# The denominator product placed directly behind the V product, and the row-maximum matmuls placed in the other slots

## The chip, the cores and the metric

The kernel runs on one core of a Trainium2 chip as one launch. The metric is device time in microseconds. The kernel before takes 3174.51 us, the median of three runs (3169.97 to 3180.08).

## The reference, cut to what matters

Four layers follow each other on 2 x 1024 tokens of width 1024, in fp32: attention, a four-stream mixing layer with Sinkhorn iterations, attention again, and an expert layer. Each layer normalises its input and adds its result to it. The change lies in the two attention layers, which compute

```python
scores = einsum('bqhd,bkhd->bhqk', q, k) / sqrt(HEAD_DIM)      # 32 query heads, 8 key heads, HEAD_DIM 32
scores = where(causal, scores, -inf)
attn = softmax(scores, axis=-1)
out = einsum('bhqk,bkhd->bqhd', attn, v)
```

A softmax needs the maximum of each row of scores, the exponentials, and their sum, the denominator.

## The kernel before, in words

Attention runs batch by batch (2), and in a batch over 8 groups. A group is one key head with its 4 query heads. A group's scores are computed twice. The first time ("S" steps, `row_scores`, L743) they lie with queries on the partitions; VectorE (DVE) takes their row maximum (`maximum`, L599 for tiles on the causal diagonal with the mask added, L602 for the others). The second time ("ST" steps, L790) they lie transposed, with the negated maximum as one more row of the product; ScalarE takes the exponential (L499), and TensorE multiplies the result by V into `ppv` ("PV" step with part 0) and by a matrix of ones into `pden` (part 1, the denominators), both on L810. Each of the two parts is 4 matmuls in the program, one for each head, 32 output columns wide and put on its own quarter of the array; the trace shows 8 records for them.

A group has 12 key tiles ("units" 0 to 11: four for the first 512 queries, eight for the second 512). The list that `iteration` writes has per unit e the steps ST e+1 half 0, ST e+1 half 1, PV e part 0, PV e part 1. All other work is hung behind one of these steps by the table `after`: eight pieces each of the projection of the next queries ("P", L722), the splitting of weights and queries ("HI", "LO", "WS"), stores, and the 38 S steps. The S steps are those of the *next* group (the row maxima must be known before its ST steps), and are spread over the units 1 to 9 in proportion to `columns`, an estimate of how much TensorE does in each step. Every engine walks the same list in the same order and takes out its own steps, so the list sets the order on each engine.

The lists are `body` (with projection and S; 6 groups of a batch), `body6` (S without projection; 1 group) and `body7` or `ahead7` (neither; the last group, `ahead7` prepares the next batch). With 2 layers and 2 batches that is 24, 4 and 4 groups. The six groups of `body` are a hardware loop of 3 turns with 2 groups each. Before the loop a prologue per batch computes keys, values and the first group's maxima.

S steps and projections write into the two banks of the tile `psh`. `bank_plan` gives each step the bank used longest ago; TensorE waits (`sh_free`) until DVE has read the step before it in that bank. Each such step is either one matmul of 512 or 384 columns, two of 256 or four of 128.

Of the kernel before, what the change touches and what calls it, by code (L numbers as in the profile page):

```python
# [30 lines left out]
BANK = 512  # L31
# [19 lines left out]
def unit_offset(e):  # L51

    qc, ki = UNITS[e]
    return max(0, ki * P - qc * BANK)
# [22 lines left out]
def columns(step):  # L77

    what, e, _ = step
    n = BANK - unit_offset(e)  # L80
    return 2 * max(n, BANK // 2) if what == "ST" else 4 * n


def iteration(full_s=True, proj=True, ahead=False):

    steps = [[("ST", e + 1, 0), ("ST", e + 1, 1), ("PV", e, 0), ("PV", e, 1)] for e in range(NU)]
    steps[-1] = steps[-1][2:]  # L90
    after = {step: [] for unit in steps for step in unit}
    first = []
    if proj:
        quarter = lambda c, i: [("P", c, k) for k in range(i * PIECES // 4, (i + 1) * PIECES // 4)]
        first = quarter(0, 0)
        for i, step in enumerate(steps[0][:3]):
            after[step] += quarter(0, i + 1)
        after[steps[0][0]] += [("WS", 0)]
        after[steps[1][1]] += [("HI", 0)]
        after[steps[2][0]] += [("LO", 0)]  # L100
        after[steps[2][0]] += [("WL", 0)]
        after[steps[5][0]] += [("RS", 0)]
        after[steps[10][1]] += quarter(1, 0)
        after[steps[10][2]] += quarter(1, 1) + [("RK", 0)]
        after[steps[10][3]] += quarter(1, 2) + quarter(1, 3)
    if full_s:
        window = [step for unit in steps[1:10] for step in unit]
        total, done, k = sum(map(columns, window)), 0, 0
        for step in window:
            done += columns(step)  # L110
            while k < len(USES) and k * total < done * len(USES) - total // 2:
                after[step] += [("S", k)]
                k += 1
        assert k == len(USES)
        after[steps[10][1]] += [("MT", 0)]
    after[steps[10][1]] += [("NORM", 0)]
    if ahead:


        for i in range(ST_):  # L120
            after[steps[i][0]] += [("XS", i)]
            after[steps[i][2]] += [("XN", i)]
            after[steps[i + 2][1]] += [("XT", i)]
            after[steps[i + 2][2]] += [("XC", i)] + [("XL", i + NX_AHEAD)] * (i + NX_AHEAD < ST_)
        first = [("XL", i) for i in range(NX_AHEAD)]
        for i in range(PIECES):
            after[steps[10][i * 3 // PIECES]] += [("P", "next", i)]
    order = [("ST", 0, 0), ("ST", 0, 1)] + ([("HI", 1), ("LO", 1), ("RS", 1)] if full_s else []) + first
    for unit in steps:
        for step in unit:  # L130
            order += [step] + after[step]
    return order + [("NORM", 1)]


# [55 lines left out]
def attention(nc, sem, layer, x_in, wqkv, cos_in, sin_in, swap, oT_d):  # L190
# [21 lines left out]
    ZT0, W0, SH0, R0, E0, PV0, AC0, N0, ST0, DMA0 = 4, 2, 1, 4, 2, 2, 2, 1, 2, 16  # L212

    pro, body, body6, body7 = prologue(), iteration(), iteration(proj=False), iteration(False, False)
    ahead7 = iteration(False, False, True)
    plan_pro, U_PRO = bank_plan(pro, spare=(2, 3, 4, 5))
    plan = {id(order): bank_plan(order)[0] for order in (body, body6, body7, ahead7)}
# [1664 lines left out]
```

How the kernel before makes its waits and increments, by code:

```python
            def load_w(n, chunk, par):  # L296
                sp.wait_ge(s["w_ready"], n + 1)
                sp.dma_start(wraw[par][:, :, :], wqkv[chunk]).then_inc(w_loaded[par], 16)
# [1 line left out]
            def store_k(b, p):  # L301
                sp.wait_ge(s["q_lo"], b * RB + 2 * p + 2)
                for part in range(2):
                    sp.dma_start(kT_d[part, ds(b, 1), p * P:(p + 1) * P, :].rearrange("o p n -> p (o n)"),
                                 stg[part][:, :].bitcast(F32)).then_inc(s["k_out"], 16)
# [1 line left out]
            def stack_queries(u, par, c):  # L308
                cols = slice(c * BANK, (c + 1) * BANK)
                for part in range(2):
                    sp.dma_start(q_d[par, part, :, cols], stg[part][:, cols].bitcast(F32)).then_inc(s["q_out"], 16)
                sp.wait_ge(s["q_out"], (u + 1) * 32)
                for row, part in enumerate((0, 1, 0)):
                    sp.dma_start(qst[par][row * HD:(row + 1) * HD, :, cols].bitcast(F32),
                                 q_d[par, part, :, cols].rearrange("(h p) n -> p h n", p=HD))\
                        .then_inc(stacked[par][c], 16)
# [6 lines left out]
            def row_max(b, g, par):  # L324
                n = b * NG + g
                sp.wait_ge(s["mT_ready"], n + 1)
                sp.dma_start(m_d[par], mT[:, :]).then_inc(s["m_out"], 16)
                sp.wait_ge(s["m_out"], DMA0 + n * 16 + 16)
                sp.dma_start(qst[par][96:97, :, :].rearrange("o h n -> o (h n)").bitcast(F32),
```

## Time and profile before

| | |
|---|---|
| median of three runs | 3174.51 us |
| the profiled execution | 3168.75 us, span 3167.0 us |
| TensorE busy | 2824.7 us (89%) |
| VectorE busy | 2122.0 us (67%) |
| ScalarE busy | 1003.6 us (32%) |
| mean granted TensorE clock | 0.935 |

Busy shares are means over five stages. The slices of the page show TensorE at nine tenths or more almost everywhere in the two attention layers (slices 2 to 13 and 21 to 34), and another picture in the mixing layer between them. So what a step of attention costs has to be read in a stretch of attention.

### The profile page before, as it was taken

The page shows a single profiled execution, that of the slowest core. Times are in us where ns is not written, and L with a number is a line of the kernel's source. Part 1 is how long each engine was busy: PE and PEld are TensorE (multiplying, and loading weights), DVE is VectorE, ACT ScalarE, POOL GpSimd, SP SyncE. Part 2 cuts the span into 40 slices and gives each one's busy share as a digit, 9 for nine tenths or more (in the row PEclk, how much of TensorE's full clock was granted, in tenths as well). Part 3 has the DMA queues.
Part 4 walks back from the last instruction along what each step waited for, and adds up shares of the span by engine and source line. Part 5 has one row for each costly group of instructions (what it writes and reads, how often), then busy time and mean ns, then how long its engine had stood idle before and what let it go on. Part 6 is the DMA issues. An engine that isn't in the chain of part 4 may idle for free. (4 is left out here: it accounts for less than half of the span.)

```text
span 3167.0 us, 48845 instructions
## 1 busy us (share of the span) xinstructions
PE 2824.7 (89%) x15824; PEld 1810.8 (57%) x15824; DVE 2122.0 (67%) x4647; ACT 1003.6 (32%) x1549; POOL 282.8 (9%) x395
## 2 busy tenths in 40 slices
PE   7999998999999799752868999989999997997999
PEld 6554454654454488652646555446554453785887
DVE  7787787777777433588776877777777784324443
ACT  2243335133344411352521434433234344201000
POOL 1011011001110000000010011010010010001111
PEclk9999999999999899765979999999999998998999
DMA  4323122323131421000133313123223120534111
GB/s 154 93 62 95 52 73 69 112 72 96 52 94 39 138 80 66 0 0 0 79 133 104 90 53 103 53 70 111 84 64 93 52 81 30 192 132 153 67 66 41
DMA packets 121071, 252.90 MB, mean 80 GB/s; under 512 B 12720, under 2 KB 39728, under 8 KB 120880
## 3 DMA queue, kind: packets, MB, share of 16 engines
q1 hardware_dynamic: 120912, 251.03, 25.1%
q8 instruction: 69, 1.13, 0.1%
q14 instruction: 90, 0.74, 0.1%
HBM read 166.57 MB, written 84.41 MB: 79 GB/s over the span
## 5 line engine op out<-in xcount | busy, mean ns | idle before, releaser
L499 ACT ACTIVATE a_prob<-a_pst 128x1024 f32<-128x1024 f32 (+3 forms) x768 | 594.5, 815 | 757.5 <-PE a_pst L790 755.2
L599 DVE CUSTOM_DVE_ANT_0 a_psh<-a_psh,a_edge 128x128 f32<-128x128 f32 (+3 forms) x1024 | 486.8, 513 | 189.1 <-PE a_psh L743 181.8
L743 PE MATMUL a_psh<-a_kst,a_qst 96*128 96x512 f32 (+3 forms) x1536 | 527.0, 404 | 40.2 <-DVE a_mx L599 20.7
L743 PEld LDWEIGHTS a_psh<-a_kst,a_qst 96*128 96x128 f32 x1536 | 263.4, 193 | 480.0 <-DVE a_mx L599 224.9
L790 PE MATMUL a_pst<-a_qst,a_kst 97*128 97x512 f32 (+2 forms) x1536 | 414.0, 372 | 28.0 <-DMA a_qst<-rowmax 10.7
L602 DVE TENSOR_REDUCE a_mx<-a_psh 128x1 f32<-128x512 f32 x512 | 343.5, 688 | 74.5 <-PE a_psh L743 67.5
L810 PE MATMUL a_ppv<-a_prob,a_vg 128*32 128x512 f32 (+3 forms) x3072 | 341.4, 518 | 13.2 <-POOL a_prob L435 11.4
L790 PEld LDWEIGHTS a_pst<-a_qst,a_kst 97*128 97x128 f32 x1536 | 278.5, 200 | 128.5 <-issue 55.5
L810 PE MATMUL a_pden<-a_prob,a_ones 128*32 128x512 f32 (+3 forms) x3072 | 335.2, 509 | 0.0
L435 POOL TENSOR_SCALAR_AFFINE_SELECT a_prob<-a_prob 128x512 f32<-128x512 f32 x256 | 178.7, 698 | 1343.0 <-ACT a_prob L499 1343.0
L646 DVE RECIPROCAL a_dens<-a_dens 128x512 f32<-128x512 f32 x64 | 214.6, 3353 | 66.9 <-ACT a_dens L507 54.5
L722 PE MATMUL a_psh<-a_xT_hi,a_w_hi 128*128 128x512 f32 x416 | 175.2, 421 | 0.6 <-DVE a_xT_lo L570 0.6
L1372 PE MATMUL h_pout<-h_w,h_o 128*128 128x512 f32 x720 | 167.7, 392 | 0.5 <-DVE h_x L1249 0.5
L722 PE MATMUL a_psh<-a_xT_hi,a_w_lo 128*128 128x512 f32 x416 | 165.5, 398 | 0.0
L722 PE MATMUL a_psh<-a_xT_lo,a_w_hi 128*128 128x512 f32 x416 | 165.4, 398 | 0.0
L1372 PEld LDWEIGHTS h_pout<-h_w,h_o 128*128 128x128 f32 x720 | 134.1, 188 | 28.5 <-DMA h_wb<-in_w_branch 0.9
L722 PE MATMUL a_pst<-a_xT_hi,a_w_hi 128*128 128x512 f32 x352 | 142.2, 404 | 6.7 <-DVE a_swp L578 4.5
L599 DVE DVE_READ_ACCUMULATOR2_ANT a_mx<- 128x1 f32 x1024 | 144.2, 141 | 0.0
L722 PE MATMUL a_pst<-a_xT_hi,a_w_lo 128*128 128x512 f32 x352 | 140.3, 399 | 0.0
L722 PE MATMUL a_pst<-a_xT_lo,a_w_hi 128*128 128x512 f32 x352 | 140.1, 398 | 0.0
L810 PEld LDWEIGHTS a_pden<-a_prob,a_ones 128*32 128x32 f32 x3072 | 73.4, 112 | 106.0 <-issue 100.3
L1455 PE MATMUL h_pout<-h_w,h_dg 128*128 x256 | 66.9, 408 | 62.7 <-ACT h_dg L1221 44.9
(212 smaller groups left out, 3798.8 us busy)
## 6 DMA issues: line engine op xcount, KB each, us to landing
a_qst<-q SPq DMA_DIRECT2D x192, 256.0 KB, 4.4
a_wraw<-in_wqkv SPq DMA_DIRECT2D x52, 512.0 KB, 5.7
q<-a_stg_hi SPq DMA_DIRECT2D x64, 256.0 KB, 2.8
q<-a_stg_lo SPq DMA_DIRECT2D x64, 256.0 KB, 3.0
oT<-a_oT SPq DMA_DIRECT2D x64, 256.0 KB, 2.5
a_kst<-kT SPq DMA_DIRECT2D x96, 128.0 KB, 3.1
h_oraw<-oT SPq DMA_DIRECT2D x16, 512.0 KB, 4.0
h_x<-in_x SPq DMA_DIRECT2D x16, 512.0 KB, 4.7
```

Source lines behind the costliest of these rows:

```text
L435: pool.affine_select(out=blk, in_=blk, compare_op=ALU.is_ge, fill=0.0, base=0, pattern=[[0, GH], [1, P]], channel_multiplier=-1)\
L499: act.activation(prob[k % 2][:, 2 * half:2 * half + 2, off:], pst[:, half, :, off:], ACT.Exp, scale=scale).then_inc(s["exp_done"], 1)
L599: part = dve.tensor_tensor_reduce(scores, scores, edge[:, BANK - n:], 1.0, 2 * MASKED, ALU.add, ALU.max, mx_hq[kc][:, h, qt:qt + 1])
L602: part = dve.tensor_reduce(mx_hq[kc][:, heads[0]:heads[0] + m, qt], psh[:, at, 0:m * n].rearrange("p (m n) -> p m n", n=n), AX.X, ALU.max)
L646: dve.reciprocal(dens[:, :], dens[:, :])
L722: mm = pe.matmul(bank(at), w[par][a][:, k, :], xT[x][:, k, c * BANK:(c + 1) * BANK], start=(i == 0), stop=(i == len(passes) - 1))
L743: mm = pe.matmul(psh[:, at, i * n:(i + 1) * n], qst[par][0:96, h, qt * P:(qt + 1) * P], kst[par][0:96, kc * BANK:kc * BANK + n], start=Tru ...
L790: mm = pe.matmul(pst[:, half, hh, off:], kst[par][0:97, ki * P:(ki + 1) * P], qst[par][0:97, 2 * half + hh, qc * BANK + off:(qc + 1) * BAN ...
L810: mm = pe.matmul(acc[h * HD:(h + 1) * HD, off:], lhs, prob[k % 2][:, h, off:], start=(ki == 0), stop=(ki == 4 * qc + 3), skip_group_check= ...
L1372: mm = pe.matmul(pout[:, half, :], o[:, par, a, k, :], w[:, b, k, half * BANK:(half + 1) * BANK], start=(i == 0), stop=(i == len(passes) - 1))
L1455: mm = pe.matmul(pout[:, par, i * C:(i + 1) * C], dg[par][:, i * (NS + 1) + n, :], rhs, start=(n == 0), stop=(n == NS), skip_group_check=True)
```

## The change

After the change a PV step with part 0 is followed at once by part 1 of the same unit, and what hung behind part 0 comes behind part 1. `open_slots` takes the slots behind part 0 out of those over which the S steps are spread, and an ST step counts half more in that spreading than before, so more S steps come behind ST steps.

```diff
     n = BANK - unit_offset(e)
-    return 2 * max(n, BANK // 2) if what == "ST" else 4 * n
+    return 3 * max(n, BANK // 2) if what == "ST" else 4 * n
+
+
+def open_slots(units):
+
+    return [step for unit in units for step in unit if step[0] != "PV" or step[2] == 1]
...
-        window = [step for unit in steps[1:10] for step in unit]
+        window = open_slots(steps[1:10])
...
     for unit in steps:
         for step in unit:
-            order += [step] + after[step]
+            if step[0] == "PV" and step[2] == 0:
+                order += [step]
+            elif step[0] == "PV":
+                order += [step] + after["PV", step[1], 0] + after[step]
+            else:
+                order += [step] + after[step]
```

TensorE in a group of `body`, from the first S step behind unit 4 to the products of unit 5, before. `a_psh<-a_kst,a_qst` is an S step, `a_pst<-a_qst,a_kst` half an ST step:

```order
L743 MATMUL a_psh<-a_kst,a_qst 128x512
...
L790 MATMUL a_pst<-a_qst,a_kst 128x512 x2
...
L743 MATMUL a_psh<-a_kst,a_qst 128x512
...
L790 MATMUL a_pst<-a_qst,a_kst 128x512 x2
...
L743 MATMUL a_psh<-a_kst,a_qst 128x128 x4
...
L810 MATMUL a_ppv<-a_prob,a_vg 32x512 x4
...
L743 MATMUL a_psh<-a_kst,a_qst 128x512
L810 MATMUL a_pden<-a_prob,a_ones 32x512 x4
...
L743 MATMUL a_psh<-a_kst,a_qst 128x512
...
L743 MATMUL a_psh<-a_kst,a_qst 128x512
```

The same place in the changed kernel (line numbers there are 10 higher):

```order
L753 MATMUL a_psh<-a_kst,a_qst 128x512
...
L753 MATMUL a_psh<-a_kst,a_qst 128x512
L798 ISA
L800 MATMUL a_pst<-a_qst,a_kst 128x512 x2
...
L753 MATMUL a_psh<-a_kst,a_qst 128x128 x4
...
L800 MATMUL a_pst<-a_qst,a_kst 128x512 x2
...
L753 MATMUL a_psh<-a_kst,a_qst 128x512
...
L753 MATMUL a_psh<-a_kst,a_qst 128x512
...
L820 MATMUL a_ppv<-a_prob,a_vg 32x512 x4
L820 MATMUL a_pden<-a_prob,a_ones 32x512 x4
```

The S step that stood between the two products is gone from there; between the pair of unit 4 and the pair of unit 5 there are now five S steps in a row of slots (2, 1 and 2 of them, with half an ST step between), where before they were spread over four slots.

The second place is unit 0 of `body`, on TensorE. Before, the last two pieces of the projection (`a_psh<-a_xT`) stand between the two products:

```order
L810 MATMUL a_ppv<-a_prob,a_vg 32x512 x4
L722 MATMUL a_psh<-a_xT_hi,a_w_hi 128x512
...
L722 MATMUL a_psh<-a_xT_hi,a_w_lo 128x512
L810 MATMUL a_pden<-a_prob,a_ones 32x512 x4
...
L790 MATMUL a_pst<-a_qst,a_kst 128x256 x2
...
L743 MATMUL a_psh<-a_kst,a_qst 128x128 x4
```

In the changed kernel they stand behind both:

```order
L820 MATMUL a_ppv<-a_prob,a_vg 32x512 x4
L820 MATMUL a_pden<-a_prob,a_ones 32x512 x4
L732 MATMUL a_psh<-a_xT_hi,a_w_hi 128x512
...
L732 MATMUL a_psh<-a_xT_hi,a_w_lo 128x512
...
L800 MATMUL a_pst<-a_qst,a_kst 128x256 x2
...
L753 MATMUL a_psh<-a_kst,a_qst 128x128 x4
```

The projection of a group thus ends one denominator product later, and the first S step comes after one half of the ST step and not after both. The order on DVE within a group stays the same.

## Rows read from the trace of the kernel before

**Rows 1.** Busy us of each engine in a group of each kind, and two other stretches.

```profile
core 0: us, PE busy (x) PEld busy (x) DVE busy (x) ACT busy (x) POOL busy (x), PEclk, DMA share, GB/s
179.19:232.91 53.72, 53.16 (x341) 27.86 (x338) 43.66 (x100) 22.20 (x31) 6.45 (x9) 1.00 0.29 81
232.91:293.09 60.18, 57.73 (x338) 30.49 (x338) 43.38 (x100) 22.61 (x31) 5.92 (x9) 0.91 0.25 66
463.00:466.00 3.00, 1.60 (x8) 0.78 (x12) 2.74 (x3) 3.00 (x5) 0.63 (x1) 1.00 0.30 89
...
250.00:258.00 8.00, 8.00 (x44) 4.46 (x37) 3.75 (x12) 3.38 (x5) 0.63 (x1) 0.50 0.72 210
```

**Rows 2.** Timeline of PE, unit 5: start us, us, engine line op, xcount.

```profile
203.79 0.56 PE L743 MATMUL a_psh<-a_kst,a_qst 96*128 96x128 f32 x4
204.28 1.06 PE L810 MATMUL a_ppv<-a_prob,a_vg 128*32 128x512 f32 x8
205.27 0.50 PE L743 MATMUL a_psh<-a_kst,a_qst 96*128 96x512 f32 x1
205.70 1.06 PE L810 MATMUL a_pden<-a_prob,a_ones 128*32 128x512 f32 x8
206.70 0.72 PE L743 MATMUL a_psh<-a_kst,a_qst 96*128 96x512 f32 x2
207.26 0.62 PE L790 MATMUL a_pst<-a_qst,a_kst 97*128 97x512 f32 x2
207.98 0.50 PE L743 MATMUL a_psh<-a_kst,a_qst 96*128 96x512 f32 x1
208.32 0.63 PE L790 MATMUL a_pst<-a_qst,a_kst 97*128 97x512 f32 x2
```

**Rows 3.** Timeline of PE in the last group of a batch (ahead7), products side by side.

```profile
546.37 1.07 PE L810 MATMUL a_ppv<-a_prob,a_vg 128*32 128x512 f32 x8
547.25 1.04 PE L810 MATMUL a_pden<-a_prob,a_ones 128*32 128x512 f32 x8
548.22 0.97 PE L790 MATMUL a_pst<-a_qst,a_kst 97*128 97x384 f32 x4
```

**Rows 4.** Timeline of DVE, the row maxima in the same group as rows 2.

```profile
204.53 0.30 DVE L599 CUSTOM_DVE_ANT_0 a_psh<-a_psh,a_edge 128x128 f32<-128x128 f32 x1 [0.32 <-PE a_psh L743]
...
205.25 0.33 DVE L599 CUSTOM_DVE_ANT_0 a_psh<-a_psh,a_edge 128x128 f32<-128x128 f32 x1
...
207.23 1.98 DVE L602 TENSOR_REDUCE a_mx<-a_psh 128x1 f32<-128x512 f32 x3 [0.73 <-PE a_psh L743]
...
210.81 0.43 DVE L599 CUSTOM_DVE_ANT_0 a_psh<-a_psh,a_edge 128x256 f32<-128x256 f32 x1 [0.56 <-PE a_psh L743]
...
211.54 2.88 DVE L602 TENSOR_REDUCE a_mx<-a_psh 128x1 f32<-128x512 f32 x4
215.25 0.57 DVE L599 CUSTOM_DVE_ANT_0 a_psh<-a_psh,a_edge 128x384 f32<-128x384 f32 x1 [0.83 <-PE a_psh L743]
```

**Rows 5.** Timeline of PE, where units of that group begin and end.

```profile
192.25 0.51 PE L743 MATMUL a_psh<-a_kst,a_qst 96*128 96x256 f32 x2 [0.38 <-DVE a_mx L599]
...
195.89 0.34 PE L743 MATMUL a_psh<-a_kst,a_qst 96*128 96x384 f32 x1
...
201.70 0.90 PE L743 MATMUL a_psh<-a_kst,a_qst 96*128 96x512 f32 x2
...
223.97 0.50 PE L743 MATMUL a_psh<-a_kst,a_qst 96*128 96x512 f32 x1
...
226.36 0.28 PE L752 MATMUL a_psh<-a_ident,a_mx 128*32 128x128 f32 x1
```

**Rows 6.** Timeline of PE at the start of a group behind the loop's branch.

```profile
245.39 0.50 PE L743 MATMUL a_psh<-a_kst,a_qst 96*128 96x256 f32 x2 [1.02 <-DVE a_swp L578]
...
247.96 0.50 PE L743 MATMUL a_psh<-a_kst,a_qst 96*128 96x256 f32 x2 [1.28 <-DVE a_mx L599]
```

**Rows 7.** Waits of PE, the whole span: who for whom, us in total, times, longest.

```profile
PE a_psh L743 <- DVE a_mx L599: 20.7, 42, 1.3
```

## The prediction

> **What bounds the kernel now.** I read the busy time of one group of each kind first, then the PE timeline inside it, then the DVE timeline beside it, then PE's waits. In a plain `body` group of 53.72 us PE is busy 53.16 us at full clock, and DVE 43.66 us [rows 1]. So TensorE is the bound, with a second engine at 81% behind it. The two are coupled by the two banks of `psh`: S step k can start only when DVE has taken the maximum of S step k-2. In the whole span PE waited for the masked maxima of L599 only 42 times, 20.7 us in all [rows 7], because the S steps are spread evenly enough. The change takes work off TensorE and bunches the S steps, so both sides have to be worked out.
>
> **What the change saves on PE.** An S step between the two products costs 0.43 us from its start to the next product (205.27 to 205.70), and two of them plus nothing else take 0.56 us to the next ST step (206.70 to 207.26) [rows 2]. A product of 512 columns that is followed by full-width work takes 1.00 us (204.28 to 205.27, 205.70 to 206.70). Side by side the first takes 0.88 us (546.37 to 547.25) and the second 0.97 (547.25 to 548.22) [rows 3], 1.85 for the pair. Split, the same work is 1.00 + 0.43 + 1.00 = 2.43 us. Joined it is 1.85, and the S step elsewhere costs 0.24 (an ordinary slot: 208.32 less 207.98 is 0.34 behind a wait, and the second S of a pair takes 0.56 - 0.34 = 0.22). That is 0.34 us less per split removed. A `body` group has ten splits (units 0, 1, 2, 4 to 10), a `body6` group eight; the last group of a batch has none. 24 x 10 + 4 x 8 = 272 splits, so 272 x 0.34 = 92 us if nothing else happened.
>
> The skill has the cause of this as a rule: by the Trainium skill, "TensorEngine Tiling (Array Packing)", section "Key Properties", changing the tiling mode drains TensorE, while the tiles of one mode run beside each other. The trace agrees with it, 1.00 against 0.88 and 0.34 against 0.22 us. By this rule alone the time would be 3169 - 92 = 3077 us; that is the first rival below.
>
> **What it costs: waits for a bank.** DVE's side first. A plain maximum (L602) starts 0.53 us after its S step (206.70 to 207.23), three of them take 1.98 us, so one starts 0.65 after the other; the S step of 207.98 is the one that needs the bank of 206.70, and it starts 1.28 us after it, 0.75 after DVE's start [rows 2, 4]. The four-head maximum starts 0.74 after its S step (203.79 to 204.53) and its last pass ends at 205.58, so it frees its bank 1.05 + 0.06 = 1.11 us after its start. The two-head one holds DVE 0.73 (210.81 to 211.54), and by the same 0.10 on top frees after 0.83. The 384-column one frees after 0.57 + 0.06 = 0.63 [rows 4].
>
> Now unit 5 as the changed list has it, with t = 0 at the first S step behind the products of unit 4. S13 at 0, S14 at 0.34, the ST half at 0.57, S15 could start at 1.04 but waits for S13's bank until 1.28 (wait 0.24). Its four matmuls take 0.49, as behind any break; ST half at 1.77, S16 at 2.24, S17 could start at 2.48. It needs the bank of S15, whose maximum starts at 1.28 + 0.74 = 2.02 and frees at 3.13: wait 0.65. S17 to the product takes 0.43, so 3.56, and the pair 1.85: the next unit begins at 5.42. Of this 0.89 us are waits, against 0.34 us that the join saved.
>
> The other units by the same ledger. Unit 6: S20 waits 0.24, S22 waits for the two-head maximum until 2.80; 5.09 us. Unit 7: waits 0.24 and 0.31; 4.82. Unit 8: S30 waits 0.46, S31 0.16, S32 0.11; 4.83. Unit 9: S35 waits 0.47; to S37 3.73. From S13 to S37 that is 23.89 us; before it was 202.04 (the second of the two at 201.70) to 223.97, 21.93 [rows 5]. So +1.96. From S6 to S13 (units 3 and 4), S8 waits 0.37, S11 0.51 and S12 0.28: 7.18 us against 202.04 - 195.89 = 6.15, +1.03. From S2 to S6 the ledger gives 3.77 against 195.89 - 192.25 = 3.64, +0.13.
>
> The start of a group: the last two projection pieces now stand behind the denominators, which puts their end 0.85 us later (1.85 - 1.00). DVE's rotation of that projection stands in front of the first maxima, and S1 and S2 already wait for DVE (0.38 at 192.25) [rows 5], so this passes on in part. Bounds 0 and 0.85, I take 0.45, for the savings in units 0 and 1 then end in a wait. The end: the last two S steps now come as a pair, so S37's maximum is done one maximum's remainder later. Before, 2.39 us lay between S37 and the transpose of the maxima (223.97 to 226.36) [rows 5]; I get 2.66, +0.27. Unit 10 has no S steps, its join is a clean -0.33. PE's other partners see nothing: ScalarE's order stays but for a few steps in `ahead7`, and its exponentials have a whole unit of 5 us to come in; the stores and loads of SP keep their slots within 2 us.
>
> Per plain group: 0.45 + 0.13 + 1.03 + 1.96 + 0.27 - 0.33 = 3.5 us. 16 of the 24 `body` groups are plain. The 8 behind the loop's branch wait for DVE at their start already (1.02 and 1.28 us [rows 6]) and then run at half clock for some 10 us (granted clock 0.50 from 250 to 258), taking 60.18 us [rows 1]. At half clock TensorE is slower than DVE's maxima, so up to S13 the joins of units 2 and 4 count (about -0.9), and then come +1.96, +0.27 and -0.33: +1.0. `body6` has neither projection nor a split in unit 10: 1.03 + 1.96 + 0.27, +3.3. Sum: 16 x 3.5 + 8 x 1.0 + 4 x 3.3 = 56 + 8 + 13 = 77 us.
>
> The profiled execution took 3168.75 us (span 3167.0 and 1.75 around it), which gives 3246. The median of the runs stands 5.8 us above the profiled one; I put 3250 us.
>
> **Bounds.** Low: if a wait costs nothing beyond itself (I charged 0.10 for the matmul behind each of some 13 waits) and DVE starts 0.1 us sooner where no product precedes the S step, a group loses about 2.2 us less, 28 x 2.2 = 60: about 3190. High: the projection's full 0.85 in 16 groups adds 6, and reads of the accumulator that I left out of the masked maxima (0.1 us each in 9 waits, 28 groups) 25: 3281. The clock is a case of its own.
>
> **Rivals.**
> *Only the drain counts.* DVE catches up in the 1.85 us of a pair, and the waits stay as small as before. For it: DVE is idle a fifth of a group, and it does catch up in the pairs. Against: the wait does not come from the sum of DVE's work but from two banks, and the bank rule shows itself at 207.98 already, with only two S steps in a row [rows 2]. Price -92 us: 3080. It decides if the waits in units 4 to 9 stay under 1.7 us a group, where I find 2.9 in units 5 to 9 and 1.2 in units 3 and 4.
> *The clock falls in the plain groups too.* With waits in every unit TensorE's granted clock could drop as it does behind the branch. Two idles of 1.02 and 1.28 us within 4 us were followed by half clock [rows 1, 6]; but in 463 to 466 PE was busy 1.60 of 3.00 us and kept the full clock [rows 1]. My waits are at most 1 us in 3. Price: the group behind the branch is 60.18 - 53.72 = 6.5 us longer, of which 1.9 are waits, so 4.6 for a long drop and under 2 for a short one; in 20 groups 40 to 90 us on top: 3290 to 3340. By the Trainium skill, "TensorE: Matmul & The Clock Gate", part 1, the clock follows how busy TensorE has been lately; that speaks for this rival, and rows 1 show both outcomes.
> *Near balance.* The DVE latencies are overestimated by a third, and waits and joins cancel: 3165 to 3185. Nothing in the rows speaks for it but that the two sums (92 saved, some 170 lost) are of one size.
>
> **Chances.** The forecast 0.66, the clock 0.16, the drain alone 0.11, near balance 0.07. The range is 3185 to 3300, which leaves out the first rival and the upper half of the second; the forecast's own range is 3190 to 3285. What a measurement of this kernel can tell from no change is about 0.3%, 10 us. Faster by more: 0.12, within: 0.05, slower by more: 0.83.
>
> **What would show it.** In the profile after: PE's wait for the masked maxima grows from 20.7 us to over 60, and that for the plain ones joins it (shown idle is smaller than my waits, as a matmul's modelled end covers some 0.15 of each); from S13 to S37 a plain group takes 23.9 us; between a V product and its denominators start to start 0.88; a plain group takes 57 us and a `body6` group some 3 us more than before; DVE's busy time stays at 2122 us and its idle grows; the mixing, projection and expert stages stay. If the plain groups come out under 53 us, the first rival holds; if their granted clock is 0.95 or less, the second has a part.

## The result and the profile after

The changed kernel takes 3249.7 us, the median of four runs (3245.8 to 3254.7), against 3172.6 for the kernel before: 1.024 of its time, 95% interval 1.0217 to 1.0263. Its profiled execution took 3249.62 us, 80.9 us more than the one of before. All of that is in the two attention layers: from the start of the program to the first output projection of the first layer it lost 42.5 us, to that of the second 80.5.

The groups of the changed kernel, in the columns of [rows 1]: a plain group, the one behind the loop's branch, and a `body6` group.

```profile
184.90:242.59 57.69, 53.15 (x342) 29.18 (x338) 43.14 (x100) 22.84 (x31) 6.23 (x9) 1.00 0.25 73
242.59:301.54 58.95, 53.06 (x337) 29.23 (x337) 42.34 (x100) 22.84 (x31) 5.93 (x9) 1.00 0.26 69
475.54:527.43 51.89, 43.96 (x293) 20.98 (x289) 37.29 (x92) 21.21 (x29) 5.47 (x9) 0.93 0.16 44
```

The plain group grew from 53.72 to 57.69 us, and PE, which was busy 53.16 of them, is now busy 53.15 of 57.69. DVE does the same work as before. So neither engine fills the group any more: each waits for the other. Busy time is no measure of the joins here: the record of a matmul runs to a modelled end, and behind a wait or a change of shape it is about 0.1 us longer (0.50 us for the first S step behind a product, 0.39 for a second one), so a part of the waiting counts as busy.

The group behind the branch became *shorter*. In the kernel before it ends where the next group's first ST step starts, at 292.99, and not at the 293.09 of [rows 1]:

```profile
232.91:292.99 60.08, 57.62 (x337) 30.39 (x337) 43.28 (x100) 22.61 (x31) 5.92 (x9) 0.91 0.25 65
```

So it took 60.08 us at a mean clock of 0.91, and takes 58.95 at 1.00 now. That does not hold for every group in this place. There are eight; five of them keep the full clock after the change (58.7 to 59.0 us), and three do not. One of the three:

```profile
905.48:966.50 61.02, 55.55 (x339) 30.66 (x338) 42.40 (x100) 22.84 (x31) 5.92 (x9) 0.94 0.23 67
```

PE's waits over the whole span, as in [rows 7]:

```profile
PE a_psh L753 <- DVE a_mx L609: 77.5, 192, 0.9
...
PE a_psh L753 <- DVE a_swp L588: 24.5, 23, 2.2
...
PE a_psh L753 <- DVE a_mx L612: 13.6, 34, 1.2
```

The wait for masked maxima went from 42 times and 20.7 us to 192 times and 77.5 us, that for the plain ones (L602 before, L612 now) from 4 times and 4.6 us to 34 times and 13.6 us, and that for the rotation at the start of a group (`a_swp`) from 8 times and 8.5 us to 23 times and 24.5 us. Inside unit 5 the timeline of PE answers to [rows 2]:

```profile
209.55 0.73 PE L753 MATMUL a_psh<-a_kst,a_qst 96*128 96x512 f32 x2
210.13 0.63 PE L800 MATMUL a_pst<-a_qst,a_kst 97*128 97x512 f32 x2
210.84 0.66 PE L753 MATMUL a_psh<-a_kst,a_qst 96*128 96x128 f32 x4
211.34 0.68 PE L800 MATMUL a_pst<-a_qst,a_kst 97*128 97x512 f32 x2
211.85 0.39 PE L753 MATMUL a_psh<-a_kst,a_qst 96*128 96x512 f32 x1
212.85 0.50 PE L753 MATMUL a_psh<-a_kst,a_qst 96*128 96x512 f32 x1 [0.61 <-DVE a_mx L609]
213.28 1.06 PE L820 MATMUL a_ppv<-a_prob,a_vg 128*32 128x512 f32 x8
214.16 1.04 PE L820 MATMUL a_pden<-a_prob,a_ones 128*32 128x512 f32 x8
215.13 0.73 PE L753 MATMUL a_psh<-a_kst,a_qst 96*128 96x512 f32 x2
```

Read it against the ledger of the prediction, whose zero is 209.55: S15 starts at 1.29 (ledger 1.28), S17 at 3.30 (3.13), the product at 3.73 (3.56), the next unit at 5.58 (5.42). The join itself is there: 0.88 us from product to product, 0.97 from the denominators on.

The marks of the same group, answering to [rows 5] (S1, S2, S6, the pair S36 and S37, the transpose):

```profile
195.85 0.50 PE L753 MATMUL a_psh<-a_kst,a_qst 96*128 96x256 f32 x2 [0.51 <-DVE a_swp L588]
...
198.69 0.50 PE L753 MATMUL a_psh<-a_kst,a_qst 96*128 96x256 f32 x2 [0.91 <-DVE a_mx L609]
...
202.43 0.34 PE L753 MATMUL a_psh<-a_kst,a_qst 96*128 96x384 f32 x1
...
233.38 0.74 PE L753 MATMUL a_psh<-a_kst,a_qst 96*128 96x512 f32 x2
...
236.40 0.27 PE L762 MATMUL a_psh<-a_ident,a_mx 128*32 128x128 f32 x1
```

### The profile page after: what moved, and what is told of

Same layout as the page of the kernel before. It is cut to its first block and busy times, and to the rows that moved or that the text cites. A ratio compares the mean times of both kernels' runs of the same rounds, so it can differ in the third digit from the quotient of the medians.

```text
span 3247.9 us, 48845 instructions
## 1 busy us (share of the span) xinstructions
PE 2799.1 (86%) x15824; PEld 1833.0 (56%) x15824; DVE 2105.5 (65%) x4647; ACT 1018.6 (31%) x1549; POOL 280.7 (9%) x395
## 3 DMA queue, kind: packets, MB, share of 16 engines
q1 hardware_dynamic: 120912, 251.03, 24.5%
## 5 line engine op out<-in xcount | busy, mean ns | idle before, releaser
L509 ACT ACTIVATE a_prob<-a_pst 128x1024 f32<-128x1024 f32 (+3 forms) x768 | 607.6, 815 | 801.8 <-PE a_pst L800 798.8
L753 PE MATMUL a_psh<-a_kst,a_qst 96*128 96x512 f32 (+3 forms) x1536 | 529.3, 401 | 137.1 <-DVE a_mx L609 77.5
L612 DVE TENSOR_REDUCE a_mx<-a_psh 128x1 f32<-128x512 f32 x512 | 339.5, 688 | 188.0 <-PE a_psh L753 182.4
L800 PE MATMUL a_pst<-a_qst,a_kst 97*128 97x512 f32 (+2 forms) x1536 | 420.6, 366 | 26.9 <-DMA a_qst<-rowmax 10.1
L820 PEld LDWEIGHTS a_pden<-a_prob,a_ones 128*32 128x32 f32 x3072 | 101.0, 113 | 157.3 <-issue 146.7
L820 PEld LDWEIGHTS a_ppv<-a_prob,a_vg 128*32 128x32 f32 x3072 | 61.7, 109 | 105.6 <-issue 67.3
```

Of the source, the lines that this page charges most:

```text
L509: act.activation(prob[k % 2][:, 2 * half:2 * half + 2, off:], pst[:, half, :, off:], ACT.Exp, scale=scale).then_inc(s["exp_done"], 1)
L612: part = dve.tensor_reduce(mx_hq[kc][:, heads[0]:heads[0] + m, qt], psh[:, at, 0:m * n].rearrange("p (m n) -> p m n", n=n), AX.X, ALU.max)
L753: mm = pe.matmul(psh[:, at, i * n:(i + 1) * n], qst[par][0:96, h, qt * P:(qt + 1) * P], kst[par][0:96, kc * BANK:kc * BANK + n], start=Tru ...
L800: mm = pe.matmul(pst[:, half, hh, off:], kst[par][0:97, ki * P:(ki + 1) * P], qst[par][0:97, 2 * half + hh, qc * BANK + off:(qc + 1) * BAN ...
L820: mm = pe.matmul(acc[h * HD:(h + 1) * HD, off:], lhs, prob[k % 2][:, h, off:], start=(ki == 0), stop=(ki == 4 * qc + 3), skip_group_check= ...
```

## The experiments

Each was run beside the kernel before on the same chip; ratios are to it. The chips differ a little from one experiment to another (the kernel before took 3172.6, 3167.8, 3168.5 and 3162.0 us beside the changed kernel, e1 to e4, e5 to e8, and e9 and e10), so runs of different batches are compared by their ratios. Group lengths are the first number of the rows of the windows, in the columns of [rows 1].

### Short row maxima: are DVE's maxima what PE waits for?

The same edit in the changed kernel (e1) and in the one before (e2):

```diff
-                if last:
...
-                        part = dve.tensor_tensor_reduce(scores, scores, edge[:, BANK - n:], 1.0, 2 * MASKED,
-                                                        ALU.add, ALU.max, mx_hq[kc][:, h, qt:qt + 1])
...
+                part = dve.tensor_reduce(mx_hq[kc][:, heads[0]:heads[0] + m, qt],
+                                         psh[:, at, 0:m * n].rearrange("p (m n) -> p m n", n=n)[:, :, 0:P // m],
+                                         AX.X, ALU.max)
```

Expected of e1:

> The changed kernel with short row maxima: each S step's maximum is one plain reduction over 128 of its columns (128, or 64 or 32 of each head) with no mask, so the maxima are not the true ones; all else, all S matmuls too, is as in the changed kernel. Theory (two banks, DVE not quick enough in a bunch): a maximum then frees its bank some 0.8 us after its S step and no S step of units 3 to 9 waits; the time falls by 7 us a plain group, to about 3050, and lies 40 to 90 us UNDER the kernel before with the same short maxima (e2). Rival (the new order costs PE something by itself, or something other than DVE's maxima releases it): it stays about 80 us ABOVE e2.

Expected of e2:

> The kernel before with the same short row maxima as e1, the control. Few S steps wait for a bank before the change, so little is to be gained: theory and rival alike expect 30 to 60 us less than the kernel before, about 3120 to 3140, most of it at the start of a group where DVE is late.

Measured: e1 2979.1 us (0.941, interval 0.939 to 0.942), e2 3025.4 us (0.955, 0.954 to 0.956). The order of the two kernels turned round: with short maxima the joined products lie 46 us under the split ones, with the true maxima 77 us above. A plain group of e1 and the one behind its branch, then the same of e2:

```profile
164.65:214.47 49.82, 49.22 (x341) 29.12 (x338) 27.01 (x58) 22.43 (x31) 6.22 (x9) 1.00 0.28 85
214.47:264.12 49.65, 49.05 (x338) 29.14 (x338) 26.66 (x58) 22.42 (x31) 5.77 (x9) 1.00 0.30 82
```

```profile
167.76:219.55 51.79, 51.79 (x341) 27.90 (x338) 27.10 (x58) 22.09 (x31) 6.43 (x9) 1.00 0.29 84
219.55:271.44 51.89, 51.79 (x337) 27.96 (x337) 27.22 (x58) 22.10 (x31) 5.47 (x9) 1.00 0.29 77
```

Only DVE's work differs from the two real kernels (27 us a group and not 43), and PE fills the group again. Joining takes 2.6 us off PE's busy time (51.79 to 49.22) and leaves 0.6 us idle, 2.0 us a group in all; the ten joins at 0.34 would give 3.4, and what became of the other 0.8 was not taken apart. The size of e2 was misjudged: 142 us less where 30 to 60 were expected. Nearly half of that lies in the eight groups behind the branch, which take 414.0 us together where they took 481.4; the one shown, 60.08 us before, takes 51.89 here at full clock. Without the long maxima their half clock does not come either.

### Joining without the new places

e3 joins every unit and leaves the weights of the spreading as before.

```diff
-            order += [step] + after[step]
+            if step[0] == "PV" and step[1] in range(12):
+                order += [step] if step[2] == 0 else [step] + after["PV", step[1], 0] + after[step]
+            else:
+                order += [step] + after[step]
```

> Denominators directly behind the V product in every unit, but the S steps are spread with the weights of before (over all four slots, those of the slot between the products then come behind both). Theory: what hurts is that five S steps must share the time between two pairs, wherever they stand in it; by the ledger of the prediction a plain group takes 58.0 us against 57.3 in the changed kernel, so 3255 to 3270 in all. Rival (the new spreading, with more S steps behind ST steps, is the culprit, and joining alone gains): 3080 to 3180.

Measured: 3293.0 us, 1.040 (1.039 to 1.042), over both expectations. The rival is out: for joined products the changed kernel's places are better than the old ones (1.024), not the culprit. A plain group at full clock is as the ledger has it, 58.07 us, 0.4 more than in the changed kernel; most of the rest is clock, as five of the twelve plain groups in the middle of the loop fell below 1.00.

```profile
183.25:241.32 58.07, 51.93 (x341) 29.00 (x338) 44.02 (x100) 22.14 (x31) 6.44 (x9) 1.00 0.26 73
...
301.84:365.54 63.70, 57.67 (x342) 31.66 (x338) 44.06 (x100) 22.51 (x31) 6.45 (x9) 0.89 0.23 66
```

The second is also a plain place in the list, but it was granted 0.89 and took 63.70.

e8 joins every unit too, with the places that the ledger of the prediction, worked through for many tables, found best for joined products. The table replaces the spreading; its rows are the units 1 to 9, its columns the four slots:

```diff
+PLACES = ((0, 1, 0, 0), (1, 0, 0, 1), (1, 1, 0, 2), (0, 2, 0, 2), (0, 6, 0, 2), (1, 2, 0, 2), (1, 2, 0, 2), (0, 2, 0, 3), (0, 2, 0, 2))
```

> All products joined as in the changed kernel, S steps placed by the best table that the ledger finds for joined products. Theory (two banks and pairs of 1.85 us do not go together, wherever the S steps stand): a plain group takes 54.9 us, 2.8 less than in the changed kernel but 1.2 more than before; in all 3175 to 3200. Rival (only the changed kernel's places were bad): below 3150.

Measured: 3200.7 us, 1.011 (1.009 to 1.013), at the upper edge of what was expected, a plain group 55.28 us. So the changed kernel's places cost some 45 us against these (77 us over the kernel before, and 32), yet with every unit joined the kernel remains slower than before. Only this one table was run for joined products; another might do better. Nor was the number of banks of `psh` varied: that two are too few is read from the ledger and from e1 and e2, where the length of the maxima was what changed.

```profile
181.17:236.45 55.28, 52.96 (x342) 29.07 (x338) 43.04 (x100) 22.36 (x31) 6.52 (x9) 1.00 0.26 76
```

### The price of one join, and of the start

e6 joins unit 10 alone, e5 unit 0 alone (the edit of e3 with `(10,)` and `(0,)`).

> The kernel before with only unit 10 joined, where no S step stands between the products, only projection pieces that nobody waits for. It isolates the price of one join with no bank wait: 24 groups x 0.30 to 0.34 us, so -7 to -8 us. Rival (joins pay nothing, the drain is hidden): 0.

Measured: 3156.1 us, 0.9965 (0.9952 to 0.9977). The two groups, plain and behind the branch:

```profile
180.25:233.60 53.35, 52.84 (x342) 28.05 (x338) 43.69 (x100) 22.19 (x31) 6.40 (x9) 1.00 0.27 79
233.60:293.38 59.78, 57.39 (x338) 30.20 (x338) 43.31 (x100) 22.61 (x31) 5.94 (x9) 0.91 0.25 68
```

0.37 us for the plain group (from 53.72) and 0.30 for the one behind the branch (from 60.08): a join that nobody's wait swallows pays what the prediction said. In all it is 12 us less than the kernel before, where 7 to 8 were expected; the interval, 7 to 15, reaches down to that.

> The kernel before with only unit 0 joined: the last two projection pieces come behind the denominators instead of between the products. It isolates the term of the group's start. Theory: in a plain group the pieces end 0.85 us later and S1, S2 wait for DVE, +0.5 to +0.7 less nothing, so 54.0 to 54.3 us against 53.7; behind the loop's branch PE waits once long and once short instead of 1.0 and 1.3 us, and the half clock that followed there stays away, as in the changed kernel: 60.1 falls to 56 to 57 us. In all -10 to -30 us. Rival (the half clock comes anyway, or the changed kernel lost it by something else): +5 to +15 us.

Measured: 3221.3 us, 1.016 (1.014 to 1.018). Both expectations failed. The first plain group is near the one forecast, 54.44; but then:

```profile
180.38:234.82 54.44, 52.87 (x341) 28.04 (x338) 43.95 (x100) 22.19 (x31) 6.44 (x9) 1.00 0.28 80
295.67:354.55 58.88, 57.30 (x341) 30.48 (x338) 44.04 (x100) 22.60 (x31) 6.45 (x9) 0.91 0.25 73
354.55:414.75 60.20, 57.44 (x341) 30.11 (x337) 43.32 (x100) 22.60 (x31) 5.93 (x9) 0.91 0.25 66
```

The second row is a plain group with half clock. Its only idle of note is one wait for the maxima, and the first group has the very same wait. Here they are on PE, in the first group and in the later one:

```profile
194.18 0.50 PE L746 MATMUL a_psh<-a_kst,a_qst 96*128 96x256 f32 x2 [1.42 <-DVE a_mx L602]
```

```profile
309.49 0.50 PE L746 MATMUL a_psh<-a_kst,a_qst 96*128 96x256 f32 x2 [1.41 <-DVE a_mx L602]
309.82 0.40 PE L793 MATMUL a_pst<-a_qst,a_kst 97*128 97x256 f32 x2
310.25 0.67 PE L746 MATMUL a_psh<-a_kst,a_qst 96*128 96x384 f32 x1
```

After the first the clock stayed (the matmul of 384 columns behind it takes 0.44 us), after the second the same matmul takes 0.67 us, and by the mean of 0.91 over 58.88 us the group ran some 10 us at half clock. What the engines did up to the end of either wait is alike, here in the last 4.2 us:

```profile
190.00:194.18 4.18, 2.77 (x27) 1.24 (x25) 4.01 (x14) 1.71 (x3) 1.15 (x1) 1.00 0.56 144
305.30:309.49 4.19, 2.78 (x27) 1.25 (x25) 4.03 (x14) 1.71 (x3) 1.15 (x1) 1.00 0.55 149
```

So one idle piece of 1.4 us was followed by half clock in one group and not in another with the same work; what decides was not settled.

e9 is the changed kernel with unit 0 split again.

```diff
-            if step[0] == "PV" and step[2] == 0:
+            if step[0] == "PV" and step[1] == 0:
+                order += [step] + after[step]
+            elif step[0] == "PV" and step[2] == 0:
```

> The changed kernel with unit 0 alone as before: its last two projection pieces stand between the products again. Isolates the group's start and its clock inside the changed kernel. By the ledger a plain group takes 0.4 to 0.7 us less (57.0 to 57.2). If the position of these pieces is what keeps the clock up behind the loop's branch (58.9 us and no half clock in the changed kernel, 60.1 to 61 with it before), half clock comes back there and the groups take 62 us or more, the whole 3260 to 3275; if the clock has another cause, 58 us there and the whole 3235 to 3245.

Measured: 3231.4 us, 1.021 (1.019 to 1.024), against 1.024 (1.022 to 1.026) for the changed kernel. By these ratios it gains some 8 us and by the plain medians 18; the intervals of the two overlap, so the gain is read from the groups.

```profile
181.87:238.77 56.90, 53.15 (x341) 28.93 (x338) 42.86 (x100) 22.86 (x31) 6.25 (x9) 1.00 0.26 74
238.77:298.52 59.75, 54.65 (x338) 29.36 (x338) 42.39 (x100) 22.86 (x31) 6.17 (x9) 0.97 0.24 68
```

A plain group gets back 0.79 us, so joining unit 0 cost it that much, nearly the 0.85 by which the join moved the pieces, and not half of it. Behind the branch the group shown has a short spell of half clock (0.97, 59.75 us). Over all eight such groups there is little between the two kernels: 475.0 us here, with a short spell in five of them, and 477.0 in the changed kernel, with a longer one in three. The expectation took it that the changed kernel has no half clock there, which is true of five groups only, and neither of its two outcomes came: the whole lies under both.

### The S steps placed by count, the products split in units 0 and 4 to 9

e4 joins unit 10 and places the S steps by a table:

```diff
-        window = [step for unit in steps[1:10] for step in unit]
...
+        k = 0
+        for e, counts in enumerate(PLACES, 1):
+            for step, count in zip(steps[e], counts):
+                after[step] += [("S", k + i) for i in range(count)]
+                k += count
...
+PLACES = ((1, 1, 0, 0), (0, 1, 0, 1), (1, 1, 0, 1), (1, 1, 2, 1), (0, 2, 2, 2), (1, 1, 2, 1), (1, 1, 2, 2), (0, 1, 2, 1), (1, 1, 2, 1))
```

> The kernel before with its products split again except in unit 10 (no S step stands there), and the 38 S steps put by a fixed table: two between the products in units 4 to 9, one or two behind the pair, at most two in one slot, one after the first ST half. By the ledger of the prediction a plain group takes 52.1 us against 53.6 before: theory 3125 to 3145. Rival (the ledger is only right where waits are long; PE's fixed costs decide): within 10 us of before.

The expectations of this part call the products split in all units (e7) or in all but 10 (e4, e10). That is not quite so. The third number of a row is the slot between the products, and it is 0 for units 1 to 3, so there too they stand side by side (in the kernel before, only those of units 3 and 11 do). Unit 1 of e4:

```profile
191.07 0.85 PE L814 MATMUL a_ppv<-a_prob,a_vg 128*32 128x384 f32 x8
191.74 0.83 PE L814 MATMUL a_pden<-a_prob,a_ones 128*32 128x384 f32 x8
```

Measured: 3100.7 us, 0.979 (0.977 to 0.980): faster than both kernels, and than expected.

```profile
180.11:232.39 52.28, 52.18 (x342) 28.04 (x338) 43.63 (x100) 22.09 (x31) 6.63 (x9) 1.00 0.28 81
232.39:286.55 54.16, 52.30 (x338) 28.15 (x338) 43.12 (x100) 22.09 (x31) 6.38 (x9) 1.00 0.27 75
```

A plain group takes 52.28 us (ledger 52.1) and PE is busy 52.18 of them. Over the 16 such groups that is some 23 us. The larger part comes behind the branch: 54.16 us instead of 60.08, at full clock, and 436.4 instead of 481.4 for all eight, of which two still have a short spell of half clock (0.97).

e7 takes that table for units 1 to 3 and nearly the old places from unit 4 on, and leaves unit 10 split; e10 takes another one, whose first S step stands behind the denominators of unit 1. In both, nothing stands between the products of units 1 to 3.

```diff
+PLACES = ((1, 1, 0, 0), (0, 1, 0, 1), (1, 1, 0, 1), (1, 0, 2, 2), (1, 1, 2, 2), (1, 1, 2, 1), (1, 1, 2, 2), (0, 1, 2, 2), (0, 1, 2, 1))
```

```diff
+PLACES = ((0, 0, 0, 2), (0, 0, 0, 0), (2, 0, 0, 2), (0, 2, 2, 1), (1, 2, 2, 2), (0, 2, 2, 1), (0, 2, 2, 1), (1, 1, 2, 1), (1, 1, 2, 1))
```

> The kernel before, all products split, with S steps placed by a table that is as in e4 in units 1 to 3 (7 of them instead of 9) and as before from unit 4 on but for single steps. It tells which part of e4's 67 us comes from the start of a group and its clock. By the ledger a plain group takes 53.0 us (before 53.6, e4 52.1). If e4's gain behind the branch (60.1 to 54.2 us, no half clock) comes from the early units, these groups take 55 us here and the whole 3115 to 3130; if not, they stay at 60 us and the whole is 3150 to 3160.

> As e4 (split except unit 10, places by table), but the first S step comes only behind the denominators of unit 1, so that no step waits for DVE's rotation, which is late behind the loop's branch. Ledger: plain 52.6 us (e4 52.25), behind the branch 53.6 (e4 54.2, two of eight 55.5 with a short half clock). Theory that the waits at the start are what brings the half clock: none is left behind the branch, and the whole is 3090 to 3105. Rival (the waits at the start don't matter): no group is faster than in e4, 3105 to 3115.

Measured: e7 3133.7 us, 0.989 (0.987 to 0.991); e10 3102.3 us, 0.980 (0.977 to 0.983). Plain and behind the branch, first e7, then e10:

```profile
178.85:232.14 53.29, 53.10 (x341) 27.79 (x338) 43.64 (x100) 22.18 (x31) 6.69 (x9) 1.00 0.28 82
232.14:288.90 56.76, 54.67 (x338) 28.32 (x338) 43.21 (x100) 22.17 (x31) 5.93 (x9) 0.97 0.25 69
```

```profile
178.65:231.44 52.79, 52.58 (x341) 28.33 (x338) 43.23 (x100) 21.99 (x31) 6.42 (x9) 1.00 0.29 80
231.44:285.35 53.91, 52.95 (x337) 28.55 (x337) 42.78 (x100) 22.08 (x31) 5.95 (x9) 1.00 0.28 75
```

e7 shows that the start of a group is worth 3.3 us to the group behind the branch (60.08 to 56.76; 31 us over the eight) and 0.4 to a plain one. Two things changed there together and were not run apart: seven S steps in units 1 to 3 where there were nine, and no S step between the products of units 1 and 2. The time of the whole lies between the two outcomes expected of it, and the groups behind the branch, at 55.2 to 56.8 us, are near the first. What e4 has beyond e7 lies in its places from unit 4 on and in the join of unit 10. e10 came out as its theory said: no half clock behind any branch. But its plain groups give back what that gains, and the two tables tie.

## Why the prediction was right

The mechanism was right: waits for a bank outweigh the joins. That the number, 3250 against 3249.7, hits so closely is luck, as terms of it missed by 16 us one way and 12 the other. By its own steps:

**TensorE is the bound and DVE stands close behind it.** Right. e1 and e2 show the coupling: with DVE's work cut from some 43 to 27 us a group, the sign of the change turns.

**A join saves 0.34 us.** Right. e6 gives 0.37 for a plain group and 0.30 behind the branch, where nobody waits for what is moved. As a sum, 92 us, it was never to be had, since the pairs need other places for the S steps.

**The waits for a bank.** Right in mechanism and nearly in size. From S2 to S6 the trace has 198.69 to 202.43, 3.74 us (ledger 3.77); from S6 to S13 202.43 to 209.55, 7.12 (7.18); from S13 to S37 209.55 to 233.72, 24.17 (23.89); from S37 to the transpose 2.68 (2.66). The 0.28 us that was short lies in the two units whose maxima are masked for several heads, 0.16 in unit 5 and 0.11 in unit 6. In unit 5 the maximum of S15, which starts at 210.84, and its last accumulator read on DVE are

```profile
211.69 0.30 DVE L609 CUSTOM_DVE_ANT_0 a_psh<-a_psh,a_edge 128x128 f32<-128x128 f32 x1 [0.31 <-PE a_psh L753]
...
212.65 0.14 DVE L609 DVE_READ_ACCUMULATOR2_ANT a_mx<- 128x1 f32 x1
```

It starts 0.85 us behind its S step and not 0.74; that is 0.11 of the 0.17 us by which S17 comes late. The other 0.06 is the read: it ends at 212.79, 0.06 behind the last pass, and S17 starts 0.06 behind the read (212.85), while I had released the bank by the pass. The prediction's "2.9 in units 5 to 9" for the sum of the waits leaves out that of S22, some 0.3 us; the lengths of the units have it.

**The start of a group.** Mis-sized: taken as 0.45 between bounds of 0 and 0.85. S2 stands 13.79 us behind the group's start now (184.90 to 198.69), and it stood 13.06 behind it before, from 179.19 [rows 1] to 192.25 [rows 5]: 0.73. e9 gives 0.79. The first and the last step of DVE's rotation of the projection, before:

```profile
188.29 0.69 DVE L577 TENSOR_TENSOR a_rot<-a_psh,a_cos 128x512 f32<-128x512 f32 x1 [0.17 <-issue]
...
190.50 0.69 DVE L582 TENSOR_TENSOR a_rot<-a_rot,a_swp 128x512 f32<-128x512 f32 x1
```

and after:

```profile
194.46 0.69 DVE L587 TENSOR_TENSOR a_rot<-a_psh,a_cos 128x512 f32<-128x512 f32 x1 [0.64 <-PE a_psh L732]
...
196.66 0.96 DVE L592 TENSOR_TENSOR a_rot<-a_rot,a_swp 128x512 f32<-128x512 f32 x1
```

The rotation starts 9.10 us behind the group's start before and 9.56 after: 0.46 later, since DVE had been busy with the splitting of weights until 188.11 and so did not need the projection earlier. That part was sized rightly. What the sum lacked is the rest, 0.27 us: the last step takes 0.96 us and not 0.69, in the plain groups of e5 too, and with unit 0 split (e9) it takes 0.69 again. GpSimd works on the probabilities at that moment, from 196.14 for 0.93 us; before, it began just behind DVE's step (190.53) and took 1.15. That the two engines hold each other up there is a guess from these rows and was not tested.

The measured parts of the plain group, in the order of the prediction's sum: 0.73 + 0.10 + 0.97 + 2.24 + 0.29 - 0.36 = 3.97 us, where it had 3.5.

**The groups behind the branch.** Wrong in sign. I forecast +1.0 us each, at half clock as before. Eight of them took 477.0 us together after and 481.4 before, -0.55 each. The long half clock did not come in five of them, and came shorter in three (mean clock 0.94). In the first, at full clock, the trace has one wait of 2.17 and one of 0.63 us where [rows 6] have 1.02 and 1.28:

```profile
255.18 0.50 PE L753 MATMUL a_psh<-a_kst,a_qst 96*128 96x256 f32 x2 [2.17 <-DVE a_swp L588]
...
257.74 0.50 PE L753 MATMUL a_psh<-a_kst,a_qst 96*128 96x256 f32 x2 [0.63 <-DVE a_mx L609]
```

**The sum.** Twelve plain groups in the middle of the loop grew by 3.9 us each and not 3.5, 47 us; the four `body6` groups 17 us and not 13; the groups behind the branch -4 and not +8; what is left, 21 us, falls on the first group of each batch and its surroundings, where 14 were forecast. 47 + 17 - 4 + 21 = 81 us, the profiled difference. The groups behind the branch were overestimated by 12 us, all others underestimated by 16.

**The rivals.** That only the drain counts was refuted by the result, and e1 shows under which condition it would have held: maxima short enough to free a bank before the third S step of a bunch. That the clock falls in the plain groups did not happen in the twelve in the middle of the loop (1.00 in all), but it was no idle fear: it did in e3 and e5. (The first groups of the last three batches stood at 0.97, two of them before the change too.) Luck had a part in it, since in e5 one wait of 1.4 us was followed by half clock. The prediction's stretch that was half idle and kept the clock [rows 1] is true of that stretch and no safe rule. Near balance did not come.

## What to carry to other kernels

When a reordering takes work off the busiest engine, write out the first few steps with the number of buffers between it and the engine that drains them: the saving counts only as long as no burst is longer than the buffers. Spread what needs draining over the slots by count and by how long each takes to drain, not by the producer's own time; here that gave 2%, with two S steps between the products of units 4 to 9 and the products side by side only where few maxima are due, while joining them everywhere lost 2.4%, and 1.1% with the other table run for it. Long idle pieces on TensorE were dearer here than they look, as some were followed by 10 us or so at half clock (e5). Moving work so that they do not arise kept the full clock (e10), but gained no more than it cost elsewhere.

## What the runs showed of the hardware that I had not expected

In e5 one idle of 1.42 us on TensorE was followed by full clock in one group and one of 1.41 by some 10 us at the lower level (1.2 and not 2.4 GHz) in the next but one. In the changed kernel 2.17 and 0.63 us of waiting in a short stretch were followed by full clock (group at 1.00), in the kernel before 1.02 and 1.28 us by the lower one (0.91); and in the group of the changed kernel at 905.48 a wait of 2.23 us was followed by the lower one (0.94). The Trainium skill, "TensorE: Matmul & The Clock Gate", part 1, tells that the clock follows how busy TensorE has been and that the point of a change varies with when the work falls; the two groups of e5 agree with that, as the work before the wait is alike in them. What it costs is in the same rows: 58.88 against 54.44 us for a group of the same work.
